# An attention and mixture-of-experts layer: the opening in another order, with three weight chunks split on VectorE and the modulation made as columns

## What is computed

```python
mod = (silu(c) @ wmod).reshape(4, 6, 1, 256)          # c is (4, 256)
sa, ca, ga, sb, cb, gb = mod[:, 0] ... mod[:, 5]
ga = sign(ga) * max(|ga|, 0.25);  gb likewise
h = layernorm(x) * (1 + ca) + sa
q, k, v = unit(h @ Wq.T + bq), unit(h @ Wk.T + bk), unit(h @ Wv.T + bv)
#   unit(y): fft(y) / (|fft(y)| + 1e-8), back to real
s = cumsum(bind(k, v), axis=1)                        # bind: product of spectra
x = x + ga * unbind(s, q)                             # times conj(fft(q))
h = layernorm(x) * (1 + cb) + sb
x = x + gb * top2_of_8_experts(h)                     # gate, swiglu, two dense layers
```

## Time and profile before

| | |
|---|---|
| median of 3 runs | 587.58 us (587.25 to 587.61) |
| the profiled execution's own time | 584.68 us |
| its span, first to last instruction | 582.5 us |
| TensorE busy, mean granted clock | 544.5 us (93%), 0.954 of full |
| VectorE busy | 473.1 us (81%) |
| ScalarE busy | 302.2 us (52%) |
| GpSimd busy | 282.8 us (49%) |
| the first half (blocks 0 to 7) | to about 240 us |
| the span by what ended last | PE 72%, DVE 13%, ACT 4%, DMA 4%, POOL 2% |

### The profile page before, as it was taken

The page is one execution under the profiler, slowest core; times in us unless marked ns, Lnnn a source line. Parts: engine busy times, 40 slices in busy tenths (PEclk is TensorE's granted clock), DMA queues, the critical chain, the costliest instruction groups (busy, mean ns, idle before and its releaser), DMA issues.

```text
span 582.5 us, 13330 instructions
## 1 busy us (share of the span) xinstructions
PE 544.5 (93%) x4008; PEld 404.8 (69%) x4009; DVE 473.1 (81%) x1062; ACT 302.2 (52%) x514; POOL 282.8 (49%) x197
## 2 busy tenths in 40 slices
PE   9999999999999985779899999999999999999992
PEld 5544555655656552537588888888888888888881
DVE  1267889999999989999688888888888888888882
ACT  4777688889797863654433333333333333333330
POOL 0004033343423342000638878877878877777634
PEclk9988999999899987858899999999999999999997
DMA  8314544644735437833677897786886686786533
GB/s 313 126 45 155 153 136 109 203 132 136 208 103 176 115 120 219 309 64 70 162 121 107 136 152 118 136 132 116 145 157 109 134 139 121 136 155 112 88 45 36
DMA packets 82109, 79.37 MB, mean 136 GB/s; under 512 B 45140, under 2 KB 71892, under 8 KB 81816
## 3 DMA queue, kind: packets, MB, share of 16 engines
q0 software_dynamic: 16912, 31.74, 31.3%
q1 hardware_dynamic: 63864, 46.28, 29.9%
q10 hardware_dynamic: 1296, 0.87, 0.5%
HBM read 44.06 MB, written 22.23 MB: 114 GB/s over the span
## 4 chain that ended last, share of the span: by engine, by line
PE 72%; DVE 13%; ACT 4%; issue 4%; DMA 4%; POOL 2%; POOLq 0%; DVEq 0%; ACTq 0%
PE ps L807 30%; PE ps L826 14%; PE ps L551 13%; PE ps L610 3%; DMA out_rows<-w_stage,region 3%; PE ps L652 2%; PE ps L564 2%; PE ps L648 2%; PE ps L474 1%; DVE region L1293 1%; POOL out_rows L1749 1%; ACT region L976 1%; PE ps L482 1%; ACT region L923 1%; DVE region L1415 1%
## 5 line engine op out<-in xcount | busy, mean ns | idle before, releaser
L807 PE MATMUL ps<-region,w_sb 128*128 128x256 f16 (+1 forms) x1920 | 194.3, 261 | 0.9 <-DMA region<-region 0.4
L807 PEld LDWEIGHTS ps<-region,w_sb 128*128 x1920 | 170.4, 98 | 20.1 <-issue 2.1
L1749 POOL DMA_INDIRECT out_rows<-w_stage,region x71 | 126.4, 1780 | 60.4 <-DMA out_rows<-w_stage,region 22.8
L1739 POOL DMA_INDIRECT region<-h_scratch,region x71 | 91.8, 1292 | 67.7 <-DVE region L1576 45.0
L1178 ACT ACTIVATE region<-region 128x1024 f16<-128x1024 f32 (+1 forms) x40 | 38.5, 961 | 130.4 <-DVE region L1630 130.4
L826 PE MATMUL ps<-region 128*128 x852 | 99.6, 273 | 1.9 <-DVE region L1636 1.7
L1622 DVE TENSOR_SCALAR region<-ps,region 128x256 f32<-128x256 f32 (+1 forms) x160 | 64.4, 448 | 43.0 <-PE ps L807 41.2
L826 PEld LDWEIGHTS ps<-region 128*128 128x128 f16 x852 | 82.6, 98 | 13.1 <-issue 3.5
L1166 ACT ACTIVATE region<-ps,region 128x256 f32<-128x256 f32 (+1 forms) x160 | 63.0, 445 | 53.0 <-PE ps L807 49.5
L551 PE MATMUL ps<-region 128*128 128x512 f32 x192 | 84.2, 595 | 3.2 <-ACT region L923 3.2
L1723 POOL TENSOR_TENSOR region<-region 128x512 f32<-128x512 f32 x30 | 37.3, 1270 | 94.9 <-DVE region L1320 94.9
(11 more groups left out here) (238 smaller groups left out, 702.3 us busy)
## 6 DMA issues: line engine op xcount, KB each, us to landing
w_stage<-in_w SPq DMA_DIRECT2D x20, 512.0 KB, 3.7
region<-in_x SPq DMA_DIRECT2D x8, 512.0 KB, 7.3
out_rows<-region SPq DMA_DIRECT2D x8, 512.0 KB, 3.0
h_scratch<-gb_bc SPq DMA_DIRECT2D x4, 1024.0 KB, 6.8
h_scratch<-region SPq DMA_DIRECT2D x8, 512.0 KB, 3.2
region<-region POOLq DMA_DIRECT2D x7, 512.0 KB, 4.5
region<-in_ramp SPq DMA_DIRECT2D x1, 2064.0 KB, 11.1
region<-in_w SPq DMA_DIRECT2D x4, 512.0 KB, 6.6
```

The lines of the kernel that those rows point to most:

```text
L807: mm = pe.matmul(ps[:, GV + 2 * half + a, (f % 2) * MT:(f % 2) * MT + wide], w, xg_t[:, s, xa * KD + k, 0:wide], start=(n == 0), stop=(n = ...
L1739: G.indirect_dma_start(out=xg_rows[:, t % XG, u, :], out_offset=None, in_=h_scratch, in_offset=bass.IndirectOffsetOnAxis(ap=idx, axis=0)). ...
L1749: G.indirect_dma_start(out=out, out_offset=bass.IndirectOffsetOnAxis(ap=scatter_idx[:, at:at + 1], axis=0), in_=y_sb[:, t % 2, u, :], in_o ...
```

## The change

Seven things, all in the opening:

1. Chunks 0 to 2 are split wholly on VectorE (`weight_chunk`: one pass for the high part, one for the low part), so their three passes on ScalarE and six low pieces on TensorE and ScalarE are gone. EARLY = 3 shifts the counts that later chunks wait for.
2. The modulation is made as columns (`modulation_columns`: 16 matmuls of four columns in one bank), copied by ScalarE, worked on by GpSimd in seven passes over 8 or 16 columns, transposed by TensorE in the middle of block 1's transform, copied by ScalarE, and stored. SP's store waits for that copy, and chunks 2 to 4 are now loaded before it.
3. Block 0's magnitudes are made one component at a time, each followed by its root; the offset is added on VectorE.
4. Block 1's first two magnitudes stand ahead of block 0's scans, the third behind them.
5. Block 1's denominator and next product, and block 2's row scales, stand ahead of block 0's `unbind`.
6. On TensorE `nyquist_cols(1)` stands ahead of `nyquist_sums(0)`; `project(2)` and eight warming matmuls stand ahead of `inverse(0)`; only pieces (1, 2) and (1, 3) are left, ahead of them.
7. On ScalarE `roots(1)` stands first in block 0's list, and `residual(0)` behind `spectra(2)` and chunk 4.

```diff
+            for n in range(5):
                 load_weights(sp, n)
-            sp.wait_ge(mod_ready, 6)
-            sp.dma_start(mod_tab, mod_rows.bitcast(I32)).then_inc(mod_out, 16)
+            sp.wait_ge(mod_copied, 2)
+            sp.dma_start(mod_tab.rearrange("m b (k q) -> (m b k) q", k=KD), mod_rows.bitcast(I32)).then_inc(mod_out, 16)
 ...
-            for n in range(2, 6):
-                load_weights(sp, n)
+            sp.dma_start(mod_flat.bitcast(I32).rearrange("p (m b d) -> p m b d", m=3, b=BATCH),
+                         mod_tab[0:3].partition_broadcast(P)).then_inc(mod_in, 16)
+            sp.dma_start(gb_bc[:].bitcast(I32), mod_tab[3, 0:2, :].partition_broadcast(P)).then_inc(gb_in, 16)
+            load_weights(sp, 5)
 ...
+            def modulation_columns():
+
+                pe.wait_ge(wmod_in, 16)
+                for m in range(4):
+                    for kd in range(KD):
+                        for ke in range(KD):
+                            at = (2 + m) * D + kd * P
+                            mm = pe.matmul(ps[:, OUT, (m * KD + kd) * BATCH:(m * KD + kd + 1) * BATCH],
+                                           wmod_sb[:, ke, at:at + P], c_silu[:, ke, :],
+                                           start=(ke == 0), stop=(ke == KD - 1))
+                mm.then_inc(mod_mm, 1)
+
             def modulation_rows():
 
-                pe.wait_ge(wmod_in, 16)
 ...
+                pe.wait_ge(mod_ready, 7)
+                pe.transpose(ps[0:MODS, OUT + 1, 0:P], mod_flat_cols, ident_sb[:]).then_inc(mod_tp, 1)
 ...
                                        start=(k == 0), stop=(k == KD - 1))
                     mm.then_inc(z_mm, 1)
+                    if t == 1 and i == 1:
+                        modulation_rows()
 ...
-                pe.wait_ge(w_hi, n + 1)
+                pe.wait_ge(w_hi, n + 1 - EARLY)
 ...
                     transform(0)
                     nyquist_cols(0)
-                    modulation_rows()
                     project(1)
-                    low_piece(0, 0)
+                    modulation_columns()
+                    continue
                 elif t == 0:
                     transform(1)
+                    nyquist_cols(1)
                     nyquist_sums(0)
-                    nyquist_cols(1)
+                    low_piece(1, 2)
                     nyquist_row(0)
-                    low_piece(1, 0)
-                    low_piece(1, 1)
+                    low_piece(1, 3)
+                    project(2)
+                    pe.wait_ge(mod_copied, 2)
+                    pe.wait_ge(w_lo[0], 2)
+                    keep_warm(8, ident_h[:], w1_sb[:, HI, 0:BLK], OUT + 1)
                     inverse(0)
-                    low_piece(1, 2)
-                    low_piece(1, 3)
                     continue
                 elif t + 1 < NBLK:
-                    project(t + 1)
+                    if t >= 2:
+                        project(t + 1)
                     transform(t + 1)
 ...
+            def modulation_columns():
+                act.wait_ge(mod_mm, 1)
+                nc.scalar.activation(mod_cols, ps[:, OUT, 0:MODS].rearrange("p (m k b) -> p m b k", m=4, k=KD),
+                                     ACT.Copy).then_inc(mod_copied, 1)
+
 ...
+                act.wait_ge(mod_tp, 1)
+                nc.scalar.activation(mod_rows, ps[0:MODS, OUT + 1, 0:P], ACT.Copy).then_inc(mod_copied, 1)
 ...
-                    if c == 2 and t == 1:
-                        split_weights(2)
                     act.wait_ge(z_ready, 6 * t + 2 * c + 2)
                     nc.scalar.activation(sq[:, c], z[:, t % 2, c, :, 0:BLK], ACT.Square).then_inc(sq_ready, 1)
+                    if t == 0 and c >= 1:
+                        first_root(c - 1)
+                    if t == 1 and c == 0:
+                        modulation_rows()
+                        split_weights(EARLY)
                     if c == 0 and t >= 3:
                         residual(t - 2)
-                if t == 1:
-                    split_weights(3)
 ...
+            def first_root(c):
+
+                act.wait_ge(mag_part, c + 1)
+                nc.scalar.activation(mag[:, 0, c, 0:BLK], mag[:, 0, c, 0:BLK], ACT.Sqrt).then_inc(root_part, 1)
+
+            def first_roots():
+
+                act.wait_ge(ny_out, 1)
+                nc.scalar.activation(mag[:, 0, :, BLK:NB], mag[:, 0, :, BLK:NB], ACT.Sqrt).then_inc(root_part, 1)
+                act.wait_ge(mag_ready, 1)
+                nc.scalar.activation(mag[:, 0, QRY, 0:BLK], mag[:, 0, QRY, 0:BLK], ACT.Sqrt).then_inc(root_ready, 1)
+
 ...
                 if t == -1:
-                    split_weights(0)
-                    roots(0)
-                    split_weights(1)
-                    modulation_rows()
+                    first_roots()
                     spectra(1)
-                    low_piece(0, 0)
+                    modulation_columns()
+                    continue
                 if t == 0:
+                    roots(1)
                     project(2)
+                    low_piece(1, 2)
                     normal_rows(2)
-                    low_piece(1, 0)
-                    low_piece(1, 1)
+                    low_piece(1, 3)
                     nyquist_row(0)
-                    roots(1)
-                    residual(0)
-                    low_piece(1, 2)
-                    low_piece(1, 3)
                     spectra(2)
                     split_weights(4)
+                    residual(0)
                     split_weights(5)
                     continue
 ...
-            def modulation():
-
-                dve.wait_ge(mod_copied, 2)
-                V.memset(z[:, 1, :, IM, BLK:NB], 0.0).then_inc(ny_zero, 1)
 ...
+            def weight_chunk(n):
+
+                dve.wait_ge(w_in[stage_of(n)], 16 * arrivals(n))
+                hi, lo = parts_of(n)
+                V.tensor_scalar(hi, staged(n), SW, None, ALU.mult).then_inc(chunk_hi, 1)
+                dve.wait_ge(chunk_hi, n + 1)
+                V.scalar_tensor_tensor(out=lo, in0=staged(n), scalar=SW, in1=hi, op0=ALU.mult,
+                                       op1=ALU.subtract).then_inc(w_lo[n % 2], 2)
+
+            def first_magnitude(c):
+
+                dve.wait_ge(sq_ready, c + 1)
+                V.tensor_tensor(mag[:, 0, c, 0:BLK], sq[:, c, RE, :], sq[:, c, IM, :],
+                                ALU.add).then_inc(mag_part if c < QRY else mag_ready, 1)
 ...
+                if t == 0:
+                    dve.wait_ge(root_part, 3)
+                    V.tensor_scalar(mag[:, s, VAL, :], mag[:, s, VAL, :], EPS_UNIT, None, ALU.add).then_inc(eps_ready, 1)
 ...
                 if t == 0:
-                    modulation()
+                    dve.wait_ge(root_ready, 1)
+                if t == 1:
+                    ln1_rows(2)
                 dve.wait_ge(den_ready, t + 1)
 ...
+                if t == 1:
+                    unbind(0)
                 dve.wait_ge(all_ready, t + 1)
                 V.reciprocal(rec, rec).then_inc(rec_ready, 1)
+                if t == 0:
+                    dve.wait_ge(mod_mm, 1)
+                    V.memset(z[:, 1, :, IM, BLK:NB], 0.0).then_inc(ny_zero, 1)
 ...
+                if t == 0:
+                    magnitudes(1, slice(KEY, QRY))
 ...
+                dve.wait_ge(sq_ready, 3 * t + parts.stop)
+                ins = V.tensor_tensor(mag[:, t % 2, parts, 0:BLK], sq[:, parts, RE, :], sq[:, parts, IM, :], ALU.add)
+                if parts.stop > QRY:
+                    ins.then_inc(mag_ready, 1)
 ...
-            for t in range(-1, NBLK):
-                if 0 <= t < NBLK:
-                    bind(t)
-                if t >= 1:
-                    residual(t - 1)
-                if t >= 0 and t + 2 < NBLK:
+            ln1_rows(1)
+            for c in range(3):
+                weight_chunk(c)
+                first_magnitude(c)
+            bind(0)
+            magnitudes(1, slice(QRY, QRY + 1))
+            nyquist_apply(0)
+            ln1_moments(2)
+            for t in range(1, NBLK):
+                bind(t)
+                residual(t - 1)
+                if t + 2 < NBLK:
                     ln1_moments(t + 2)
 ...
-                if t == -1:
-                    ln1_rows(1)
-                    magnitudes(0)
 ...
+            def modulation():
+
+                pool.wait_ge(mod_copied, 1)
+                g = mod_each[:, 0::3, :]
+                G.tensor_scalar(mod_sign, g, 0.0, 2.0, ALU.is_ge, ALU.mult).then_inc(mod_ready, 1)
+                G.tensor_scalar(mod_each[:, 2, :], mod_each[:, 2, :], 1.0, SX, ALU.add, ALU.mult).then_inc(mod_ready, 1)
+                G.tensor_scalar(mod_each[:, 1, :], mod_each[:, 1, :], SX, None, ALU.mult).then_inc(mod_ready, 1)
+                pool.wait_ge(mod_ready, 1)
+                G.tensor_scalar(mod_sign, mod_sign, -1.0, None, ALU.add).then_inc(mod_ready, 1)
+                pool.wait_ge(mod_ready, 4)
```

(7 more changed lines are left out.)

90 lines of the change are left out of this document (35 added, 55 removed).

## The result

**593.22 us** (median of 4 executions, 592.45 to 594.51) where the kernel before took 587.41 (587.15 to 587.61): ratio 1.0101, 95% interval 1.0083 to 1.0120. The forecast was 587.9 with a range of 583.4 to 589.8: wrong, too low by 5.3 us. The profiled execution took 593.23 us, span 591.4, of which TensorE was busy 549.6, VectorE 480.0, ScalarE 295.5 and GpSimd 289.9; the mean granted clock fell from 0.954 to 0.933. The two spans differ by 8.9 us, but the profiled execution of before lies 2.9 us under the median of its kernel, so 5.8 us, the difference of the medians, is what needs a cause.

The account below looks back on a forecast made before the run. TensorE was taken to set the pace from block 2's transform on, so the change was worth that start's shift, 66.47 to 66.8, +0.3 us; added to the median of 587.58 this gave 587.9 us, range 583.4 to 589.8.

Parts of the forecast that it names:

- start of block 2's transform: The one instant whose shift was taken as the change's worth: 66.8 us forecast, against 66.47 in the kernel before.
- What bounds it, and where the change is worth something: From block 2's transform on TensorE sets the pace, so only that transform's start matters; further VectorE lead buys nothing.
- Its work from there is the same in both kernels: Claim that TensorE's work from block 2's transform on is unchanged, and its later waits move with it.
- TensorE up to block 1's transform: Opening on TensorE: low clock, columns 7.2 us, block 1's transform from 38.9, 1.7 us earlier, until 52.0.
- Rival 2: Weight loads not slowed by the low clock: columns take 3.6 us, block 2 at 64.8, 585.9 us; chance 0.15.
- VectorE up to the scans: Block 0 on VectorE: reciprocal's end near 36.3, square of block 1 at 50.3, scans' end at 53.9.
- The gain of 6.4 us ends in this wait: VectorE's reciprocal ends near 36.3 instead of 42.7, but the lead is lost waiting for ScalarE's second square of block 1.
- GpSimd's small passes: Seven modulation passes on GpSimd from 39, 0.45 us each, 3.2 in all, with ends 0.8 and 5.9.
- just covered at every end: GpSimd's modulation passes finish before TensorE wants them, a third into block 1's transform, at about 44.9.
- From the scans to block 2: Denominator and row scales 58.0, ScalarE's rows 60.1, transposes 61.0, then warming and inverse; block 2's transform at 66.2 to 68.8.
- The high end needs each low stretch at its longest; I take 66.8.: Block 2's transform placed between 66.2 at full clock and 68.8 with transposes and warming low; 66.8 chosen, +0.3 us.
- Rival 1: Longest low stretches, in block 1's transform and the warming products: block 2 at 68.3 to 68.8, 589.4 to 589.9; chance 0.25.

Follow-up runs that it names:

- e11: e6 with block 2's moments moved ahead of block 0's third magnitude and idle products placed by the gaps seen; 583.14 us, ratio 0.9961 to the kernel before.
- e5: Changed kernel with block 2's moments and row scales made in VectorE's 6 us wait for block 1's squares; 587.74 us, ratio 0.9981 to the kernel before.
- e8: The changed kernel again, no edit, 11 executions on another chip; 591.91 us, ratio 1.0048 to the kernel before.
- e3: Changed kernel with the 16 column products spread through block 0's transform; 589.30 us, ratio 1.0012 to the kernel before.
- e4: Kernel before with only its first three weight chunks split on VectorE, modulation rows kept; 591.86 us, ratio 1.0052 to the kernel before.
- e2: Changed kernel with the warming products moved ahead of block 2's transposes and made 22; 589.99 us, ratio 1.0018 to the kernel before.
- e10: e9 with four more idle products behind block 1's Nyquist columns; 584.46 us, ratio 0.9885 to the kernel before.
- e12: e10 with four more idle 512-wide products ahead of block 1's transposes; 584.04 us, ratio 0.9968 to the kernel before.
- e1: Changed kernel without the eight warming products ahead of block 0's inverse; 589.76 us, ratio 1.0017 to the kernel before.
- e6: Changed kernel with the edits of e3 and e5, and warming divided, 12 products ahead of block 2's transposes and 6 behind; 586.97 us, ratio 0.9976 to the kernel before.
- e9: Changed kernel with the edits of e7 and e5 and twelve idle products ahead of the inverse; 588.17 us, ratio 0.9940 to the kernel before.
- e7: Changed kernel with seven idle 512-wide products between pairs of column products and the transposition behind the fifth piece; 589.47 us, ratio 1.0002 to the kernel before.

## Why the prediction was wrong

The forecast was +0.3 us and the medians differ by 5.8. Of that 4.7 is the start of block 2's transform, sized at 66.8 and measured at 71.14: this is the term that failed, in two of its steps below. The rest, 1.1 us, came behind block 2, where the sum had nothing.

*What bounds it, and where the change is worth something: half right.* TensorE's waits in blocks 2 to 7 stayed small, and most of the loss is there at block 2's start. But "Its work from there is the same in both kernels" was wrong about the duration: 126.7 us from block 2's transform to block 7's, against 124.8, with two low stretches that before's profile lacks. Over all 14 profiles that distance goes with the number of low stretches in it: 124.8 with one (before), 125.4 to 126.4 with two, 126.7 to 128.0 with three. It does not go with the lead: e11 starts block 2 at 62.4 and needs 125.4, the changed kernel starts it at 71.1 and needs 126.7. And behind block 7's start, which no edit touches, the 14 profiles differ by 5.4 us, from 391.3 (before) to 396.7 (e5), with no cause found. The start of block 2 is therefore not the whole of what an execution takes.

*TensorE up to block 1's transform: right.* Forecast 38.9, measured 38.17, with the columns at 6.83 us (taken 7.2); the transform ran low until 44.0 and ended at 52.2 (52.0). Rival 2, weight loads not slowed by the clock, is refuted: all 32 loads of the columns took 333 to 337 ns in the low stretch, where the earlier trace rows has 189 at the full clock. What was overlooked is that the fall itself moves from execution to execution, so that this was a draw among cases and not one number. In e8's profile the clock fell at 32.9 and was low for 6.8 us, into the transform, which started at 35.0 all the same; no rival had that.

*VectorE up to the scans: right.* Reciprocal's end 36.04 (forecast 36.3), the wait for the square until 50.67 (50.3), the scans' end 54.2 (53.9). "The gain of 6.4 us ends in this wait" holds: the wait was 6.04 us, and in e5 the moments and row scales fit into it with 2.24 left.

*GpSimd's small passes: at the upper bound.* 5.9 us of passes, 6.4 with the gaps, where 3.2 was taken and 5.9 was the end; "just covered at every end" missed by a stall of 0.35 us (1.00 and 1.37 in e8 and e5, where block 1's transform starts at 35.0). The 0.45 taken for each lies between what they took beside VectorE's reciprocal (0.20 to 0.31 in e3) and beside its products (0.56 to 1.24).

*From the scans to block 2: this step failed.* I wrote "denominator and row scales 58.0", then ScalarE's rows 60.1. The denominator started on time, at 57.12, but took 1.83 (taken 0.70), the scales 0.17 and 1.02 (about 0.35 taken for both), and the rows ended 2.1 us late, at 62.2. GpSimd's products and basis took 5.71 and 2.21, 1.3 us more than the rows of before, where less of VectorE's work lay beside them. The working itself had GpSimd's products there, from 54.0 on, and still took each pass at its shortest: the denominator from a row in which GpSimd was idle, the scales from the kernel before, where they lay beside GpSimd's products too but met the end of one.

The traces show what such a pass waits for. In the kernel before and then in the changed one, the four-element pass and one of GpSimd's four products:

```profile
55.22 0.17 DVE L1272 SCALAR_TENSOR_TENSOR region<-region 128x4 f32<-128x4 f32 x1
55.33 1.26 POOL L1723 TENSOR_TENSOR region<-region 128x512 f32<-128x512 f32 x1
```

```profile
58.36 1.71 POOL L1786 TENSOR_TENSOR region<-region 128x512 f32<-128x512 f32 x1
```

In before the pass began 0.1 us ahead of the next product's start at 55.33 and took 0.17. In e4 it began 0.3 us ahead of one (52.14, product at 52.46) and took 0.38. In the changed kernel it began 1.0 us ahead of the last product's end (59.07, end 60.07) and took 1.02, done at 60.09. The three durations are what was left of the product beside it. The denominator pass likewise began at 57.12, and 0.6 us behind the product's start at 58.36 it was over; that product took 1.71, not about 1.25. Both engines lose, and a duration depends on the instant.

e5 shows the place: with the scales made while GpSimd is idle, the wait ahead of the transposes shrinks from 4.67 to 0.34, and the median is 4.2 us under the changed kernel's.

*The low clock there: the wrong end taken.* "The high end needs each low stretch at its longest; I take 66.8." Behind a wait of 4.67 us on TensorE both transposes (1.97) and warming (3.62) ran low: together 2.8 us more than the 1.04 and about 1.75 of the full clock, which is what the working had as its high end, 68.8. With rows that are 2.1 late that makes 71. Rival 1, the longest low stretches, is what happened, at both of its places, and only its price was short, by the late rows and by what came behind block 2: 589.4 to 589.9, measured 593.22. I gave it a chance of 0.25, when the gap ahead of the transposes was in my own working: pieces over by 57, transposes at 60.

*The size.* Given the first four executions the change costs 1.0%; given the 11 of e8, on another chip, 0.5% (0.1 to 0.9), and in e8's profile block 2 starts only 1.0 us behind before's. So how much of the 5.8 us the program always pays is not settled, and a range for it should have held several cases. What the first magnitudes by component, and the columns with their turning as against the rows, are each worth was not measured apart.

## What to carry to other kernels

Price a short pass of VectorE beside GpSimd's products by what is left of the product beside it, not by a row in which it happened to be short: the same four-element pass took 0.17, 0.38 and 1.02 us. Move what a later stage needs into an earlier wait of the same engine: in e5 the wait that it had caused disappeared, and the low clock over transposes and warming with it. Thin products (few columns) stood better between dense ones than in a row (e3, e11), by the instants. Idle products gained where they filled a wait or stood ahead of the fall (e2, e10, e12) and lost where they ran low in front of the work (e1), by the instants too; what they are worth in the whole time no pair of runs shows by itself. And compare a dozen executions on one chip, not four, before a difference of 1% is given a cause.

## What was not expected of the hardware

- VectorE beside GpSimd, each instruction of the same shape: 516-wide fused pass 1.83 against 0.70 us, and 1.64 against 0.70 for the next one; a fused pass of 4 elements 1.02, 0.38 and 0.17, each time over where GpSimd's product was, while the reciprocal of 4 elements just ahead of it took 0.17 or 0.18 all three times. GpSimd's passes of 8 to 16 elements took 0.56 to 1.24 beside VectorE's products in the changed kernel, against 0.20 to 0.31 beside its reciprocal in e3; the longest is as long as one of VectorE's 1032-wide passes (1.23). VectorE's statistics passes over 256 elements did not change: four took 1.40 beside GpSimd's products in the changed kernel and 1.40 with GpSimd idle in e6. That the neighbour is the cause is read from these coincidences; the 1.83 stands in every profile of the changed order (1.82 to 1.85). No run took GpSimd's work away.
- The granted clock falls at different instants in executions of one program (30.4 and 32.9 in the changed kernel), and with it 32 four-column products take 6.83 or 4.66 us. One kernel (e9) spread over 15 us, on a chip where the kernel before spread over 5.7.
- Idle products behind the fall do not bring the clock back by their number alone: seven among 32 thin products left it low for 13.7 us, while in e7's execution the same instructions, entered at the high clock, ran at it throughout.
